# Mixture-of-experts code sum by an identity matmul and a two-part single-pass map, in a planned single-core kernel

## The chip, the core and the metric

The kernel runs on one core of a Trainium2 chip. The metric is the time of the whole program on the device in microseconds, as the median of several executions. The core has five engines with an instruction queue each: TensorE (PE in the profile, its weight loads PEld), VectorE (DVE), ScalarE (ACT), GpSimd (POOL) and SyncE (SP), which here only issues DMAs. Each queue is worked off in order, and the engines meet through semaphores.

## What is computed

Eight batches of 512 tokens with 256 features pass through four residual layers: a local attention A over 44 offsets, a feed-forward part F, a full causal attention B, and F again. The change touches F alone. Its core in the reference, with M = 64 code columns, E = 8 experts and H = 512:

```python
spikes_enc = jax.nn.sigmoid(inputs_embeds @ enc_W + enc_b)
cont = flat @ s2c_W + s2c_b
...
h = jax.nn.relu(jnp.einsum('nm,emh->enh', cont, We1) + be1[:, None, :])
expert_out = jnp.einsum('enh,ehm->enm', h, We2) + be2[:, None, :]
output_flat = jnp.einsum('enm,ne->nm', expert_out, gates)
spikes_moe = jax.nn.sigmoid(output_flat @ c2s_W + c2s_b).reshape(b, s, H)
decoded = jax.nn.sigmoid(spikes_moe @ dec_W + dec_b)
```

The gates are zero for all but two of the eight experts. The line with `c2s_W` is called "mapped to the code" here: 64 columns go to 512.

## The kernel before

**Calls.** A call is one stage for one batch: 8 calls of A, 8 of B and 16 of F. The attention calls run in the order A0, A1, B0, A2, B1, A3, and so on to B6, B7 (`calls`, from line 327). The F call with number n belongs to the n-th attention call and is interleaved with attention call n+1. So the F calls 1, 3, 5, 7, 9, 11 and 14 run beside a B call, as does 13; the F calls 0, 2, 4, 6, 8, 10 and 12 run beside an A call; F call 15 is the last and has nothing beside it.

**The order is planned.** `ordered()` simulates the engines with a price in us for each block of work (`p.put` in `local_phases`, `causal_phases`, `expert_phases`) and writes out one fixed queue for each engine. At each step it takes the block that can start first, within a tick of `TICK` us, and among equals the one with the least `urgency`: its offset of `PULL` and `CALL_PULL` less `DEPTH` times the length of the chain behind it. So these tables decide which call's work stands where on PE, DVE and ACT, and which of the eight PSUM banks each product gets.

**An F call.** The input x is normalised and transposed (`turn`), `enc` makes t_enc (tanh form of the sigmoid, four products of 128 rows), `cont` makes the 64 code columns twice, one copy in rows 0 to 63 and one in rows 64 to 127. ACT writes `cont` and `cont_hi`, which is `cont` in the type fp32r, and DVE writes `cont_lo = cont - cont_hi` (line 1434). The 16 `hid` products take two matmuls each, `(w, cont_hi)` and `(w, cont_lo)`; `we1` holds the rounded weights in its upper 64 rows and the rest of them in its lower 64. `eo` forms two experts at a time, one in each half of the 128 rows; DVE multiplies by the gates (line 1448) and adds up (line 1453) into `moe`, still two half sums, one above the other. `c2s` then is four products with plain fp32 operands, `c("c2s_w", n * P, P)` of 128 rows (the 64-row weights stacked twice, so that the two halves are added in the product) against `moe`; ACT takes the tanh (line 1170). `dec` (line 1800) starts when the four tanh tiles are there, 16 fp32 products in each of two banks; it ends in tanh, a second normalisation and the sum into x (`close`, lines 1470 and 1475).

**Setup.** Inside A0, DVE prepares constants (`setup_`, from line 1481): `split` makes the two parts of `we1` from `setup_pack`. Two packs of constants come by DMA at the start, `kept_pack` (stays) and `setup_pack` (lies in arena F until F call 0).

## Time and profile before

| what | value |
|---|---|
| median of 3 runs | 1747.21 us (1744.1 to 1747.36) |
| profiled execution | 1746.18 us, span 1743.3 us |
| PE busy | 1591.9 us, 91% |
| PEld busy | 895.6 us, 51% |
| DVE busy | 1285.2 us, 74% |
| ACT busy | 785.6 us, 45% |
| granted TensorE clock, mean | 0.98 |
| idle PE from 250 to 1450 us | 1200 - 1146.7 = 53.3 us |

The profiled execution lasts 2.9 us longer than its span, from the first to the last instruction. Busy time of PE is the union of its instructions, whose ends are modelled: they overlap, and the pace is read from one start to the next. In a row, the number in brackets after an instruction is the idle time of its engine just before it and what ended it. A product of two fp32 operands stands in the trace as two MATMUL instructions; one with fp32r operands as one.

### The profile page before, as it was taken

Reading aid. Unit: us, or ns where it says so; the run is one execution under the profiler, and the core shown is the slowest. Engines: PE = TensorE matmul, PEld = TensorE weight load, DVE = VectorE, ACT = ScalarE, POOL = GpSimd, SP = SyncE. Lnnn points to the kernel's source line nnn. Section 1 sums busy time; section 2 is a strip of 40 time slices with the busy share of each in tenths; the row PEclk is TensorE's granted clock in tenths of the full one; section 3 lists DMA queues with packets and bytes.
Section 4 is the critical chain, followed back from the end, with each engine's and each line's share of the span. In section 5 each row is a group of like instructions: output and inputs, shape, how many; then the busy total and the mean of one; then the engine's idle time right before and its main releaser. Section 6 shows DMA issues by size and latency. Waiting matters only on the chain. (4 is left out here: it accounts for less than half of the span.)

```text
span 1743.3 us, 28682 instructions
## 1 busy us (share of the span) xinstructions
PE 1591.9 (91%) x10784; PEld 895.6 (51%) x10800; DVE 1285.2 (74%) x3138; ACT 785.6 (45%) x1473; POOL 137.1 (8%) x155
## 2 busy tenths in 40 slices
PE   4689899999999989999999999999999998998976
PEld 2163564545555365554755456553655546454533
DVE  5969867896679866798668966898667985646723
ACT  1043445535364444644355353644436443563633
POOL 1020110001101020000100011010200001000000
PEclk9899999999999999999999999999999999998989
DMA  9040350014301152021600134001520216004000
GB/s 325 18 158 14 138 167 2 16 73 158 99 2 48 40 186 71 4 87 63 194 2 16 73 138 119 2 29 59 182 74 4 87 51 189 7 11 138 13 3 12
DMA packets 50262, 133.98 MB, mean 77 GB/s; under 512 B 6256, under 2 KB 22576, under 8 KB 45520
## 3 DMA queue, kind: packets, MB, share of 16 engines
q1 hardware_dynamic: 50128, 132.16, 23.0%
q8 instruction: 88, 1.44, 0.3%
q14 instruction: 46, 0.38, 0.1%
HBM read 80.99 MB, written 46.04 MB: 73 GB/s over the span
## 5 line engine op out<-in xcount | busy, mean ns | idle before, releaser
L1308 DVE TENSOR_TENSOR arena_AB<-qT,kT 128x2048 f32<-128x2048 f32 (+3 forms) x240 | 399.4, 1715 | 9.4 <-PE bank L1606 5.0
L1363 DVE CUSTOM_DVE_ANT_0 bank<-bank,causal_b 128x512 f32<-128x512 f32 (+3 forms) x512 | 233.6, 523 | 130.7 <-PE bank L1680 130.2
L1524 PE MATMUL bank<-arena_F,kept 128*128 128x512 f32 (+1 forms) x544 | 255.9, 615 | 13.9 <-DVE arena_F L1453 9.5
L1606 PE MATMUL bank<-arena_AB,slot_w 128*32 128x512 f32 x1408 | 200.0, 614 | 34.0 <-DVE arena_AB L1308 32.1
L1120 ACT ACTIVATE arena_AB<-bank 128x512 f32<-128x512 f32 (+1 forms) x352 | 166.9, 586 | 78.3 <-PE bank L1694 78.3
L1524 PEld LDWEIGHTS bank<-arena_F,kept 128*128 128x128 f32 (+1 forms) x544 | 99.6, 192 | 140.4 <-issue 117.1
L1153 ACT ACTIVATE arena_F<-bank,kept 128x512 f32<-128x512 f32 x256 | 160.4, 705 | 18.1 <-PE bank L1524 16.1
L1800 PE MATMUL bank<-kept,arena_F 128*128 128x256 f32 x512 | 116.2, 381 | 6.6 <-ACT arena_F L1170 6.6
L1785 PE MATMUL bank<-arena_F,kept 128*64 128x512 f32 x512 | 119.4, 600 | 2.2 <-ACT arena_F L1153 1.0
L1524 PE MATMUL bank<-xnT,kept 128*128 128x512 f32 x256 | 115.5, 604 | 4.4 <-ACT xnT L1045 2.7
L988 POOL TENSOR_TENSOR rstd_F<-var_eps_F,minus_half 128x4 f32<-128x4 f32 x32 | 34.3, 1072 | 971.3 <-DVE var_eps_F L1238 971.3
L1692 PE MATMUL bank<-arena_AB 99*128 99x256 bf16 (+3 forms) x512 | 110.2, 301 | 0.2
L1524 PE MATMUL bank<-cont_hi,we 128*128 128x512 f32 x256 | 108.6, 424 | 1.4 <-DVE arena_AB L1363 0.7
L1800 PEld LDWEIGHTS bank<-kept,arena_F 128*128 128x128 f32 x512 | 95.1, 189 | 25.9 <-ACT arena_F L1170 6.9
L1606 PEld LDWEIGHTS bank<-arena_AB,slot_w 128*32 128x32 f32 x1408 | 35.4, 109 | 133.2 <-DVE arena_AB L1308 86.6
L1524 PE MATMUL bank<-cont_lo,we 128*128 128x512 f32 x256 | 100.5, 393 | 0.0
L1711 PE MATMUL bank<-arena_AB,V_b 128*32 128x512 f32 (+3 forms) x1024 | 85.9, 438 | 10.5 <-ACT arena_AB L1120 7.6
L1694 PE MATMUL bank<-causal_T,ident_b 128*128 128x128 bf16 x512 | 95.2, 219 | 0.0
L1680 PE MATMUL bank<-arena_AB 96*128 96x512 bf16 (+3 forms) x512 | 85.7, 301 | 2.2 <-DVE arena_AB L1363 1.4
L1461 DVE TENSOR_TENSOR arena_F<-bank,kept 128x512 f32<-128x512 f32 x32 | 22.0, 688 | 88.5 <-PE bank L1800 88.5
L1071 ACT ACTIVATE arena_AB<-bank,kept 128x512 f32<-128x512 f32 (+1 forms) x48 | 33.6, 701 | 115.9 <-PE bank L1613 115.9
L1137 ACT ACTIVATE arena_F<-bank,half_enc_b 128x512 f32<-128x512 f32 x64 | 44.0, 687 | 92.1 <-PE bank L1524 92.1
(191 smaller groups left out, 2420.9 us busy)
## 6 DMA issues: line engine op xcount, KB each, us to landing
arena_AB<-band SPq DMA_DIRECT2D x32, 1344.0 KB, 6.4
arena_AB<-stacks SPq DMA_DIRECT2D x64, 384.0 KB
stacks<-arena_AB SPq DMA_DIRECT2D x48, 256.0 KB, 2.8
band<-arena_AB SPq DMA_DIRECT2D x32, 328.0 KB, 3.6
stacks<-xnT SPq DMA_DIRECT2D x32, 256.0 KB, 2.6
band<-kT SPq DMA_DIRECT2D x4, 1352.0 KB, 22.0
stacks<-xn SPq DMA_DIRECT2D x16, 256.0 KB, 2.4
kept<-kept_pack SPq DMA_DIRECT2D x1, 3797.0 KB, 18.7
```

The lines of the kernel that those rows point to most:

```text
L1120: nc.scalar.activation(p_T[:, n % RS, cols[0]:cols[-1] + 1, 0:w], ps[:, 0:len(cols) * w].rearrange("p (c q) -> p c q", c=len(cols)), ACT.E ...
L1153: nc.scalar.activation(hid[:, n % RH, :], ps[:], ACT.Relu, bias=c("be1", n, 1)).then_inc(read, 1)
L1308: ins = nc.vector.tensor_tensor(prod[SET_AT[i]][:, col:col + c, :], qT[:, hf, :].unsqueeze(1).broadcast_to([P, c, T]), k, ALU.mult)
L1363: ins = nc.vector.tensor_tensor_reduce(out=s, in0=s, in1=causal[:, (TT - 1 - i) * P:T], scale=-1.0, scalar=BIG, op0=ALU.add, op1=ALU.min, ...
L1524: ins = nc.tensor.matmul(out(ps), w, x, start=n == 0, stop=n == len(pairs) - 1)
L1606: ins = nc.tensor.matmul(ps[HS * col:HS * (col + 1), :], slot_w[:, slot(n), :], prod[SET_AT[i]][:, col, :], start=r == 0, stop=False, skip ...
L1680: ins = nc.tensor.matmul(ps[:, at:at + (i + 1) * P], stacks[0:K, h // 4, 0, h % 4, i * P:(i + 1) * P], stacks[0:K, h // 4, 1, h % 4, 0:(i ...
L1692: nc.tensor.matmul(ps[:, at * w:(at + 1) * w], stacks[0:K + 3, g, 1, col, k * P:(k + 1) * P], stacks[0:K + 3, g, 0, col, k * P:T], start=T ...
L1694: ins = nc.tensor.matmul(ps[:, at * w:at * w + P], ident_b[:], causal_T[:], start=False, stop=True, skip_group_check=True)
L1711: ins = nc.tensor.matmul(ps_o[HS * col:HS * (col + 1), k * P:T], V_b[:, k, columns_of(4 * g + col)], p_T[:, n % RS, col, 0:w], start=k == ...
L1785: ins = nc.tensor.matmul(ps[M * e:M * (e + 1), :], we2[:, 2 * n + e, k, :], hid[:, (4 * n + 2 * e + k) % RH, :], start=k == 0, stop=k == 1)
L1800: ins = nc.tensor.matmul(ps[:, i * D:(i + 1) * D], t_moe[:, k, at:at + P], dec_w[:, k, :], start=k == 0, stop=k == KF - 1)
```

## The change

- `c2s_w` moves from the pack that stays to the setup pack, behind `we1`. A new tile `by_cont` holds `we1` and `c2s_w` side by side, and `split` treats both: upper 64 rows rounded, lower 64 rows the rest.
- A new phase `both` stands before `c2s`. PE multiplies `moe` by `pair_sum`, a 128 x 128 matrix of four identities of 64, as a plain fp32 product; each half of the result holds the sum of the two half sums. ACT copies the result to `cont_hi` (fp32r), DVE subtracts: `cont_lo = result - cont_hi`.
- Each `c2s` product is now two matmuls with fp32r operands, `(w, cont_hi)` and `(w, cont_lo)`. The first waits until DVE has read the bank of `both`.
- `ones` moves to the end of arena F; two small additions of `ident` make `pair_sum` in the setup.
- The planner has the new blocks, and `TICK`, `DEPTH`, `PULL` and `CALL_PULL` are other numbers, so that the order of all stages is planned anew.

```diff
-    ("be1", 2 * E), ("we2", E * 2 * M), ("be2", E // 2), ("c2s_w", FF), ("c2s_b", KF),
+    ("be1", 2 * E), ("we2", E * 2 * M), ("be2", E // 2), ("c2s_b", KF),
...
-          ("causal_T", P), ("we1", E * EH)]
+          ("causal_T", P), ("we1", E * EH), ("c2s_w", FF)]
...
-        p.put(("c2s", m), ("PE", 0.86, ("eo", E // 2 - 1, "DVE")), ("ACT", 0.6))
+        if m == 0:
+            p.put("both", ("PE", 0.86, ("eo", E // 2 - 1, "DVE")), ("ACT", 0.6), ("DVE", 0.67))
+        p.put(("c2s", m), ("PE", 0.46, ("both", "DVE")), ("ACT", 0.6))
...
-TICK, DEPTH = 0.078, 0.23
+TICK, DEPTH = 0.02, 0.04
...
-    ("A", "ACT"): {"sT": 730},
-    ("A", "DVE"): {"prod": 2330},
-    ("A", "PE"): {"tS": 1545.8, "pA": -2110, "pr": -630},
-    ("B", "DVE"): {"S": 1140, "pr": 330},
-    ("B", "PE"): {"turn": 1070, "S": 2980, "ST": 590, "pr": 230},
-    ("F", "ACT"): {"hid": 1230},
-    ("F", "DVE"): {"lg": 2160, "eo": -1470},
-    ("F", "PE"): {"turn": 740, "hid": 983.2, "dec": 4990},
+    ("A", "ACT"): {"p": -40},
+    ("A", "DVE"): {"prod": 3260, "tS": 400, "pr": -850},
+    ("A", "PE"): {"prod": 590, "pA": 342.5, "on": 470, "oNT": 1520, "pr": 341},
+    ("B", "DVE"): {"S": 1010},
+    ("B", "PE"): {"v": 180, "S": 2390, "ST": 600},
+    ("F", "ACT"): {"hid": 630, "c2s": -2050},
+    ("F", "DVE"): {"lg": 460, "both": 1320},
+    ("F", "PE"): {"turn": 1890, "hid": 1070, "gb": -1370, "eo": -290, "c2s": 190, "dec": 6710},
...
-    "A": [-4050, 2690, 0, 0, -446.1, 0, 0, 0],
-    "B": [0, 0, 0, 0, 0, 0, -630, 0],
-    "F": [0, 0, 0, 0, 0, 0, 109.2, 0, 0, 0, 0, 0, 0, -1500, 0, 0],
+    "A": [-6150, 0, -860, 0, 0, 0, 0, 0],
+    "B": [0, 0, 0, 0, 0, 0, 0, -410],
+    "F": [-350, 0, 0, 0, 0, 0, 0, 0, 0, 0, 0, 0, 0, -570, 160, 0],
...
+                elif kind == "both":
+                    act.wait_ge(*bank_full(u, name))
+                    nc.scalar.copy(cont_hi, place(u, name)[0][:]).then_inc(sem["F"]["moe_hi_ready"], 1)
...
+                elif kind == "both":
+                    dve.wait_ge(*nth(u, "moe_hi_ready", 1))
+                    ps, read = place(u, name)
+                    nc.vector.tensor_tensor(cont_lo, ps[:], cont_hi.bitcast(fp32), ALU.subtract).then_inc(read, 1)
...
+                    for half in range(2):
+                        once(nc.vector.tensor_tensor(pair_sum[:, half * M:(half + 1) * M], ident[:, 0:M], ident[:, M:P], ALU.add))
...
-                    we1_flat, rounded = we1[:].rearrange("p e n -> p (e n)"), arena["F"][:, SETUP_W:SETUP_W + E * EH]
-                    once(nc.vector.tensor_copy(rounded.bitcast(fp32r), s_only("we1")))
-                    once(nc.vector.tensor_copy(we1_flat[0:M, :], s_only("we1")[0:M, :]))
-                    once(nc.vector.tensor_tensor(we1_flat[M:P, :], s_only("we1")[M:P, :], rounded[M:P, :], ALU.subtract))
+                    given, rounded = setup_only[:, S_W:SETUP_W], arena["F"][:, SETUP_W:2 * SETUP_W - S_W]
+                    once(nc.vector.tensor_copy(rounded.bitcast(fp32r), given))
+                    once(nc.vector.tensor_copy(by_cont[0:M, :], given[0:M, :]))
+                    once(nc.vector.tensor_tensor(by_cont[M:P, :], given[M:P, :], rounded[M:P, :], ALU.subtract))
...
+                elif kind == "both":
+                    pe.wait_ge(*nth(u, "moe_ready", 1))
+                    product(u, name, lambda ps: ps[:], [(pair_sum[:], moe)])
                 elif kind == "c2s":
                     if n == 0:
-                        pe.wait_ge(*nth(u, "moe_ready", 1))
-                    product(u, name, lambda ps: ps[:], [(c("c2s_w", n * P, P), moe)])
+                        pe.wait_ge(*bank_read(u, "both"))
+                    w = c2s_w[:, n * P:(n + 1) * P]
+                    product(u, name, lambda ps: ps[:], [(w, cont_hi), (w, cont_lo)])
```

## Rows read from the trace of the kernel before

**Rows 1.** The page, busy time, share and instructions of each engine.

```profile
PE 1591.9 (91%) x10784; PEld 895.6 (51%) x10800; DVE 1285.2 (74%) x3138; ACT 785.6 (45%) x1473; POOL 137.1 (8%) x155
```

**Rows 2.** Windows: length, busy PE, PEld, DVE, ACT, POOL (instructions), clock, DMA, GB/s.

```profile
250.00:1450.00 1200.00, 1146.71 (x7737) 646.40 (x7748) 930.72 (x2258) 575.01 (x1082) 91.99 (x97) 1.00 0.22 72
1450.00:1680.00 230.00, 203.61 (x1417) 118.24 (x1417) 143.34 (x509) 109.35 (x216) 12.61 (x15) 0.95 0.18 54
1680.00:1743.30 63.30, 44.74 (x154) 24.05 (x155) 18.24 (x48) 22.25 (x39) 1.01 (x1) 0.88 0.02 9
```

**Rows 3.** Groups by line and form: busy us, mean ns, idle before.

```profile
L1524 PE MATMUL bank<-arena_F,kept 128*128 128x512 f32 x512 | 238.8, 615 | 12.5 <-DVE arena_F L1453 9.5 <-issue 1.5 <-ACT arena_F L1045 1.4
L1434 DVE TENSOR_TENSOR cont_lo<-arena_F,cont_hi 128x512 fp32r<-128x512 f32 x16 | 10.9, 684 | 17.1 <-ACT cont_hi L1143 17.1
L1143 ACT ACTIVATE cont_hi<-bank,s2c_bias 128x512 fp32r<-128x512 f32 x16 | 10.9, 680 | 0.0
```

**Rows 4.** Windows, finished moe to first dec: F calls 4, 5, 14 and 15.

```profile
616.95:621.80 4.85, 3.70 (x9) 1.47 (x9) 4.25 (x10) 3.46 (x6) 0.58 (x1) 1.00 0.95 372
706.84:720.46 13.62, 13.28 (x101) 6.78 (x99) 9.35 (x41) 8.96 (x19) 0.00 (x0) 1.00 0.00 1
1624.10:1637.95 13.85, 13.74 (x97) 6.83 (x96) 13.71 (x60) 8.38 (x16) 0.00 (x0) 1.00 0.02 5
1719.88:1724.62 4.74, 3.71 (x9) 1.47 (x9) 0.00 (x1) 2.75 (x4) 0.00 (x0) 1.00 0.00 0
```

**Rows 5.** Timeline, F call 5: start, us, engine, line, instruction.

```profile
706.98 3.65 PE L1524 MATMUL bank<-arena_F,kept 128*128 128x512 f32 x8
...
710.47 0.33 PE L1692 MATMUL bank<-arena_AB 99*128 99x384 bf16 x1
```

**Rows 6.** Timeline, F call 4 beside A3, around its c2s.

```profile
614.11 1.44 PE L1581 MATMUL bank<-kept,arena_AB 128*128 128x128 f32 x12
...
617.00 3.70 PE L1524 MATMUL bank<-arena_F,kept 128*128 128x512 f32 x8 [1.45 <-DVE arena_F L1453]
617.35 1.08 DVE L1264 TENSOR_REDUCE arena_AB<-bank 128x8 f32<-128x352 f32 x2
...
621.80 3.71 PE L1800 MATMUL bank<-kept,arena_F 128*128 128x256 f32 x16 [1.09 <-ACT arena_F L1170]
625.34 1.97 PE L1626 MATMUL bank<-kept,arena_AB 128*128 128x128 f32 x16
```

**Rows 7.** Timeline, F call 0, two hid products.

```profile
184.01 0.50 PE L1524 MATMUL bank<-cont_hi,we 128*128 128x512 f32 x1
...
184.34 0.39 PE L1524 MATMUL bank<-cont_lo,we 128*128 128x512 f32 x1
...
184.57 0.40 PE L1524 MATMUL bank<-cont_hi,we 128*128 128x512 f32 x1
...
184.83 1.27 ACT L1153 ACTIVATE arena_F<-bank,kept 128x512 f32<-128x512 f32 x2 [1.02 <-PE bank L1524]
```

**Rows 8.** Timeline, F call 15: c2s, its first tanh, first dec.

```profile
1719.94 3.70 PE L1524 MATMUL bank<-arena_F,kept 128*128 128x512 f32 x8 [1.62 <-DVE arena_F L1453]
...
1721.10 0.69 ACT L1170 ACTIVATE arena_F<-bank,half_c2s_b 128x512 f32<-128x512 f32 x1 [4.94 <-PE bank L1524]
...
1724.62 7.17 PE L1800 MATMUL bank<-kept,arena_F 128*128 128x256 f32 x32 [0.98 <-ACT arena_F L1170]
```

**Rows 9.** Timeline, F call 15: from cont_hi to cont_lo.

```profile
1698.04 0.68 ACT L1143 ACTIVATE cont_hi<-bank,s2c_bias 128x512 fp32r<-128x512 f32 x1
...
1698.82 0.69 DVE L1434 TENSOR_TENSOR cont_lo<-arena_F,cont_hi 128x512 fp32r<-128x512 f32 x1 [17.07 <-ACT cont_hi L1143]
```

**Rows 10.** Timeline, setup: the three instructions of split.

```profile
89.00 1.23 DVE L1497 CAST arena_F<-arena_F 128x2048 fp32r<-128x2048 f32 x1
...
90.27 1.52 DVE L1498 CAST we<-arena_F 64x2048 fp32r<-64x2048 f32 x1
...
91.82 2.59 DVE L1499 TENSOR_TENSOR we<-arena_F 64x2048 fp32r<-64x2048 f32 x1
```

More of the change, by code:

```diff
@@ L446, in fills_of @@
     if stage == "F":
-        reader = "DVE" if kind in ("lg", "eo", "dec") else "ACT"
+        reader = "DVE" if kind in ("lg", "eo", "dec", "both") else "ACT"
         return [phase], reader
@@ L606 @@
 ATTN_SETUP = 11
-DVE_SETUP = 26
+DVE_SETUP = 28
 PARITY = ("_even", "_odd")
@@ L655, in build @@
         cont_lo = sb("cont_lo", [P, T], fp32r)[:]
-        we1 = sb("we1", [P, E, EH], fp32r)
+        by_cont = sb("by_cont", [P, E * EH + FF], fp32r)
+        we1 = by_cont[:, 0:E * EH].rearrange("p (e n) -> p e n", e=E)
+        c2s_w = by_cont[:, E * EH:E * EH + FF]
         rh = sb("rh", [P, T])
         gT = sb("gT", [P, T], bf16)
+        pair_sum = sb("pair_sum", [P, P])
         V = sb("V", [P, TT, VW])
@@ L750, in build @@
         setup_only = arena["F"][:, 0:SETUP_W]
+        ones = arena["F"][:, ARENA["F"] - P:ARENA["F"]]
         Norm = namedtuple("Norm", "xn xnT stats mv var rstd scrap")
```

5 lines of the change are left out of this document (2 added, 3 removed).

## The prediction, before the result was known

> **What bounds the kernel now.** I read the busy shares first. PE leads with 91% against 74% for DVE and 45% for ACT [rows 1]. A share is only an average, so the windows came next. From 250 to 1450 us PE is busy 1146.7 of 1200 us, which is 95.6%, at a granted clock of 1.00 [rows 2]; DVE has 930.7 us there. The reader is to see that two thirds of the program are held by PE with 53 us of small holes in them, and that the last 63 us, in which F call 15 runs alone, are another thing: PE busy 44.7 of 63.3 us, DVE 18.2, ACT 22.3 [rows 2]. There each step waits for the one before, and what counts is the length of the chain.
>
> The Trainium skill, "Perfetto Trace Analysis", section "Identifying the Most-Contended Engine", says that the busy share of matmuls is a poor measure of how near TensorE is to its limit, and asks for the busy share of weight loads instead; that is 51% here. Taken alone it would say that half of PE is free.
>
> Then I looked at the place of the change in all 16 calls, from the moment at which `moe` is complete to the first `dec`. There are two kinds, and the last call. **Covered calls**: in F call 5 PE is busy 13.28 of 13.62 us [rows 4]; `c2s` is followed at once by scores of B [rows 5], and `dec` comes 10 us later. Calls 3, 7, 9 and 11 look the same, calls 1 and 13 nearly so, and call 0 has the transposes of A1 in between: eight calls. Call 14 is covered too, but there DVE is full with 13.71 of 13.85 us [rows 4]. **Open calls**: in F call 4 PE waits 1.45 us in its queue for `moe`, runs `c2s`, waits again 1.09 us for the tanh tiles and runs `dec` [rows 6]; the window is 4.85 us long with 3.70 us of PE [rows 4]. Calls 2, 6, 8, 10 and 12 look the same: six calls. Call 15 has a window of 4.74 us with 3.71 us of PE [rows 4, 8].
>
> **Pace and prices.** The eight MATMULs of `c2s` last from 706.98 to the next product at 710.47, 3.49 us or 0.87 us for a plain fp32 product of 512 columns [rows 5]; the mean of 615 ns for one MATMUL [rows 3] is longer than the pace because they overlap. A matmul with fp32r operands follows the last at 184.57 - 184.34 = 0.23 us, the first of a group takes 0.33 us [rows 7]. So PE loses 3.49 us per call and gets 0.87 us for `both` and 8 x 0.23 + 0.1 = 1.94 us for the new `c2s`: 2.81 us, **0.68 us less per call**, 10.9 us in 16 calls. DVE gets 0.68 us and ACT 0.68 us per call, at the prices of `cont_lo` and `cont_hi` [rows 3]; ACT's copy might be some 0.1 us cheaper, which changes nothing.
>
> **The new waits.** PE now cannot go from `moe` to `c2s` directly. From the start of `both` to ACT is 1721.10 - 1719.94 = 1.16 us [rows 8]; from ACT to DVE 1698.82 - 1698.04 = 0.78 us, DVE 0.69 us [rows 9], and 0.06 us to PE, as from the end of `moe` at 1719.88 [rows 4, 8]. `c2s` starts 2.69 us after `both`. Its first tanh starts 184.83 - 184.01 = 0.82 us later [rows 7] and four of 0.69 us follow [rows 8], because PE now delivers every 0.46 us and ACT needs 0.69. With 0.25 us to PE, `dec` can start 2.69 + 0.82 + 2.76 + 0.25 = 6.5 us after `both`, against 1724.62 - 1719.94 = 4.7 us now [rows 8]: **1.8 us more of chain**. In it PE has two holes, 2.69 - 0.87 = 1.8 us before `c2s` and 6.5 - 2.7 - 1.9 = 1.9 us after it. Queued behind the waiting `both` on DVE is whatever the plan puts there: maxima of B's scores in covered calls, in open calls the softmax of A (two reductions start at 617.35, half a microsecond after `moe` [rows 6]), on ACT the exponentials of the same stage. A copy placed too early holds those up, placed too late it lengthens the hole.
>
> **Covered calls, eight:** B's scores and weightings are there to fill both holes, as they fill the 10 us before `dec` today. I take the full 0.68 us less 0.05 us for one more change between kinds of matmul, -0.63 x 8 = **-5.0 us**. The bounds are nothing gained and -0.7 each. In call 14 DVE gets as much as PE loses; I take 0, bounds +0.7 and -0.7.
>
> **Open calls, six:** PE has 3.7 us of holes where it has 1.1 us now. If nothing fills them, the call costs +1.8 us, the chain's own growth. The next work of A in the queue is a set of transposes of 1.97 us, at 625.34, directly behind the first half of `dec` [rows 6]; its data comes by DMA, so it may be ready for the second hole and not for the first. If it fills the second hole, the sum is 3.7 - 1.9 - 1.1 - 0.68 = 0.0 us. If the transposes of 1.44 us at 614.11 [rows 6] also go into the first hole, it is -1.4 us, but the softmax that waits for them is on A's way through the DMA. The offsets are set anew, so the plan has a chance at all of it; I take -0.3 us each, near the middle case, **-1.8 us**, with bounds -8.4 and +10.8.
>
> **Call 15:** nothing lies beside it, **+1.8 us**, taken in full.
>
> **Setup:** `split` works on 2560 columns instead of 2048: a quarter more of 1.23 + 1.52 + 2.59 = 5.34 us is +1.3 us on DVE [rows 10], and two additions of 64 columns add about 0.3 us. It stands ahead of a softmax of A0 and PE has little else then; I take **+1.2 us**, bounds 0 and +1.6. The move of 256 KB from one pack to the other costs nothing: the sum of the bytes ahead of the setup is the same, and DVE reads this pack at 89.00 with no idle time before it [rows 10]. Were it late, 262 kB at the 372 GB/s of rows 4 would be 0.7 us. `ones` in arena F and the names cost nothing; `both` holds one of eight banks 2.7 us, which only the plan feels.
>
> **The offsets anew:** they move the work of every stage. The trace cannot show their effect. The 53 us of holes in the middle [rows 2] bound what they can give, and one hole more or less of 1 us in each of eight rounds makes 8 us either way. I take 0 and keep -8 and +8.
>
> **Sum:** -5.0 + 0 - 1.8 + 1.8 + 1.2 = -3.8 us on the profiled execution's 1746.18 us, 1742.4 us. The median of the runs stands 1.0 us above that execution and the fastest run 2.1 us below, so I leave the median at 1742.4 us, 0.3% less than 1747.21. About 0.2%, 3.5 us, is what a measurement of this kernel can tell from no change.
>
> **Rivals.**
> *All holes filled* (chance 0.24): the plan finds work for both holes of the open calls. -0.68 x 8 - 1.4 x 6 + 3.0 = -10.8, about 1735 us. For it: PE is at 95.6% already with a fixed plan. Against: the open calls have a hole of 1.1 us that nothing fills today, although 2 us of transposes stand behind `dec` [rows 6].
> *Open holes stay open* (0.16, the other side): no work of A is ready between `both` and `dec`, six calls cost 1.8 us each. -5.0 + 10.8 + 3.0 = +8.8, about 1755 us. It decides from the point at which the band's DMA lands later than 4.5 us after `both`. DMA is at 0.95 in just this window [rows 4], which speaks for it.
> *PE's saving does not reach the end* (0.14): in the covered calls DVE and ACT, which get 0.68 us each and are busy 9.35 and 8.96 of 13.62 us [rows 4], hold the pace, and PE only idles longer. -1.8 + 3.0 = +1.2, about 1748 us. The rule of the skill named above points this way. The trace speaks against it: PE stands idle 0.34 of 13.62 us there [rows 4], starts follow each other without a gap at 0.43 us per fp32 MATMUL, and a weight load lies under a running matmul.
> *The clock falls* (0.03): in the last 63 us the mean granted clock is 0.88, that is 63.3 x 0.12 x 2 = 15 us at 1.2 GHz [rows 2], which cost up to 7.6 us; PE had stood idle before the calls' chain there. If a hole of 1.8 us did the same in each open call at half that price, +23 us, about 1765 us. The windows of rows 4 say 1.00 with 1.1 us holes. The Trainium skill, "TensorE: Matmul & The Clock Gate", section "A second HAM failure mode: psum-queue depth-cycling", describes small idles between groups of matmuls that make the clock swing; the trace shows no such swing at the present holes.
> *The two parts are no single passes* (0.02): if the new matmuls ran at 0.43 us instead of 0.23, 128 of them would cost 25 us more, about 1767 us. The `hid` products of the same types at 0.23 us [rows 7] exclude nearly all of it.
>
> **How the numbers follow.** The forecast, 1742.4, has the remaining 0.41; by the offsets' bounds its own range is 1734 to 1750. For 8 in 10 I reach to the filled case and into the open one: 1730 to 1755. Faster by over 0.2% means under 1743.7: all of the filled case and some two thirds of the forecast, less where its offsets turn out badly, 0.53. Within 0.2%, 1743.7 to 1750.7: a quarter of the forecast and most of the third rival, 0.24. Slower: open holes, clock, passes and a bad plan, 0.23.
>
> **What would show it.** New rows for `pair_sum` x32 MATMULs and for `c2s` x128 at a pace of 0.23 us; PE's busy time lower by some 11 us; in covered calls B's matmuls between `both` and `c2s`; in open calls A's transposes between `c2s` and `dec`; in call 15 6.5 us from `both` to `dec`; `split` at 6.7 us. PE idle between 250 and 1450 us well above 53 us would make it wrong, and so would a softmax of A that waits behind `both` on DVE.

## The result and the profile after

The changed kernel takes 1775.37 us (median of 4 runs, 1772.95 to 1779.09), the kernel before, beside it, 1747.28 us: a ratio of 1.0157 with an interval of 1.0137 to 1.0177. It is 28 us slower, where 1742.4 us was forecast, and it lies outside the range of 1730 to 1755. The profiled execution took 1779.09 us with a span of 1777.1 us.

The busy times, from the page of after, beside [rows 1]:

```profile
PE 1605.2 (90%) x10816; PEld 913.9 (51%) x10832; DVE 1300.1 (73%) x3156; ACT 794.5 (45%) x1489; POOL 139.7 (8%) x155
```

The matmuls are 32 more, as they should be (32 for the pair product; 128 single ones in place of 128 halves of fp32 products). PE's busy time should have fallen by 11 us. It rose by 13.3 us. The middle window of after, beside [rows 2] (length, busy time of PE, PEld, DVE, ACT and POOL, granted clock, DMA share, GB/s):

```profile
250.00:1450.00 1200.00, 1133.84 (x7621) 643.91 (x7631) 926.71 (x2248) 568.17 (x1068) 91.17 (x94) 0.98 0.21 68
```

From 250 to 1450 us PE is idle for 66.2 us where it was 53.3, which was one of the signs named as making the prediction wrong. And the granted clock is 0.98 where it was 1.00 [rows 2]. Read in windows of 50 us, the stretch has some 37 us at 1.2 GHz where it had 7; the whole execution has 1777.1 x (1 - 0.969) x 2 = 110 us of it, where it had 70. PE's busy time grows because the same matmuls last longer.

The new groups of after (busy us, mean ns, idle before), beside [rows 3]:

```profile
L1538 PE MATMUL bank<-arena_F,pair_sum 128*128 128x512 f32 x32 | 18.6, 664 | 13.7 <-DVE arena_F L1461 7.4 <-DMA arena_AB<-band 6.3
L1538 PE MATMUL bank<-cont_hi,by_cont 128*128 128x512 f32 x320 | 139.0, 434 | 5.3 <-DVE cont_lo L1469 3.5 <-DVE arena_AB L1371 1.3
L1469 DVE TENSOR_TENSOR cont_lo<-bank,cont_hi 128x512 fp32r<-128x512 f32 x16 | 11.0, 688 | 11.5 <-ACT cont_hi L1174 11.4
L1174 ACT CAST cont_hi<-bank 128x512 fp32r<-128x512 f32 x16 | 9.6, 599 | 35.8 <-PE bank L1538 35.8
```

PE now stands idle 13.7 us ahead of the 16 pair products; ahead of the old `c2s` it was 9.5 us, the part of the 12.5 us of [rows 3] that ended with the last addition (L1453). So this stall has moved to `both` and has grown. DVE's subtraction costs 0.69 us, as forecast, and ACT's copy 0.60 us, the 0.1 us less that the prediction had thought possible.

**A covered call of after**, F 5, timeline, beside [rows 5]:

```profile
718.03 1.07 PE L1538 MATMUL bank<-arena_F,pair_sum 128*128 128x512 f32 x2
719.15 0.58 ACT L1174 CAST cont_hi<-bank 128x512 fp32r<-128x512 f32 x1 [0.26 <-PE bank L1538]
719.76 0.69 DVE L1469 TENSOR_TENSOR cont_lo<-bank,cont_hi 128x512 fp32r<-128x512 f32 x1 [1.92 <-ACT cont_hi L1174]
720.70 0.48 PE L1538 MATMUL bank<-cont_hi,by_cont 128*128 128x512 f32 x1
...
722.41 0.39 PE L1538 MATMUL bank<-cont_lo,by_cont 128*128 128x512 f32 x1
...
726.80 3.71 PE L1818 MATMUL bank<-kept,arena_F 128*128 128x256 f32 x16
```

`c2s` starts 2.67 us after `both` and PE has work of B in between, `c2s` lasts 722.41 - 720.70 + 0.23 = 1.94 us. The prediction had 2.69 and 1.94.

**An open call of after**, F 6 beside A4, PE and DVE; F 4 of before stands in [rows 6]:

```profile
828.07 0.83 PE L1595 MATMUL bank<-kept,arena_AB 128*128 128x128 f32 x6
830.99 1.12 PE L1538 MATMUL bank<-arena_F,pair_sum 128*128 128x512 f32 x2 [2.09 <-DMA arena_AB<-band]
833.26 3.65 PE L1640 MATMUL bank<-kept,arena_AB 128*128 128x128 f32 x16 [1.14 <-issue]
834.07 1.09 DVE L1272 TENSOR_REDUCE arena_AB<-bank 128x8 f32<-128x352 f32 x2 [3.13 <-DMA band<-arena_AB]
836.06 0.68 DVE L1469 TENSOR_TENSOR cont_lo<-bank,cont_hi 128x512 fp32r<-128x512 f32 x1
836.80 0.80 PE L1538 MATMUL bank<-cont_hi,by_cont 128*128 128x512 f32 x1
837.39 0.63 PE L1538 MATMUL bank<-cont_lo,by_cont 128*128 128x512 f32 x1
...
841.18 7.17 PE L1818 MATMUL bank<-kept,arena_F 128*128 128x256 f32 x32 [1.14 <-ACT arena_F L1178]
```

From `both` to `dec` it is 10.2 us, where the prediction's chain had 6.5. F 6 is one of the two longest: the six open calls take 7.3, 7.8, 10.2, 8.3, 10.2 and 8.6 us here, and 4.6 to 4.8 in before. Three things are to be seen. PE stands idle 2.09 us ahead of `both`; the row names a DMA, but the band read had nothing to do with `both`, which waits for DVE's last addition (it ended at 830.94). On DVE the softmax of A (L1272) stands ahead of the low part (L1469) and itself waits 3.13 us for a DMA, so the high part, ready at 832.73, lies unused for 3.3 us. PE meanwhile waits 1.14 us for A's band and then transposes it (L1640); `c2s` stands behind these transposes in its queue. And the passes of `c2s` last 0.63 us where they last 0.39 in F 5, and the next one starts 0.43 us later, not 0.23: PE runs at half its clock.

Read over whole calls, from the first `enc` tile to the last tanh, the open call F 6 and the covered call F 7, first before, then after:

```profile
776.80:836.40 59.60, 57.24 (x322) 28.86 (x322) 45.73 (x64) 27.56 (x49) 3.20 (x4) 1.00 0.25 90
876.30:931.90 55.60, 54.88 (x302) 30.77 (x305) 39.51 (x146) 30.35 (x59) 0.00 (x0) 1.00 0.01 2
```

```profile
786.00:849.80 63.80, 59.04 (x317) 31.04 (x317) 44.74 (x61) 28.60 (x51) 3.08 (x4) 0.95 0.24 88
892.70:948.70 56.00, 54.68 (x305) 30.60 (x308) 39.00 (x142) 30.90 (x59) 0.00 (x0) 1.00 0.01 3
```

The open call grew by 4.2 us, with 0.05 x 63.8 x 2 = 6.4 us at 1.2 GHz in it; the covered one, which has 0.68 us of matmuls less, did not shrink.

**The round.** From F 4 to F 12 the program repeats a round of one open call, A, one covered call and B, four times. Each number below is the mean of the four rounds, between the same instructions' ends in each kernel's trace: the round, the open call and the covered call (first `enc` tile to last tanh), PE's idle time, and the time at 1.2 GHz.

| kernel | round | open | covered | PE idle | 1.2 GHz |
|---|---|---|---|---|---|
| before | 204.1 | 59.0 | 55.8 | 9.2 | 1.7 |
| filled_holes_before | 203.4 | 59.0 | 55.8 | 9.3 | 0.0 |
| after | 209.4 | 62.7 | 55.7 | 11.8 | 8.5 |
| new_sum_old_order | 209.0 | 64.0 | 56.2 | 11.0 | 10.2 |
| filled_holes_old_order | 205.7 | 61.1 | 56.1 | 8.5 | 0.0 |
| split_in_covered_only | 203.8 | 59.1 | 56.1 | 9.5 | 0.0 |
| split_without_first | 203.8 | 59.1 | 56.1 | 9.4 | 0.0 |
| covered_passes_alone | 202.4 | 59.1 | 54.5 | 9.4 | 0.9 |
| old_sum_new_order | 207.2 | 61.3 | 55.7 | 10.7 | 3.4 |
| old_sum_in_place | 210.3 | 60.8 | 60.0 | 11.6 | 6.8 |
| old_sum_write_first | 210.4 | 64.5 | 55.7 | 13.1 | 6.8 |
| write_before_read | 209.3 | 64.0 | 55.8 | 13.1 | 6.0 |
| low_part_first | 209.9 | 63.2 | 55.7 | 12.9 | 6.0 |
| filled_holes_new_order | 207.6 | 62.0 | 55.7 | 9.1 | 0.9 |
| filled_holes_both_moves | 208.7 | 62.9 | 55.9 | 10.5 | 0.9 |
| new_sum_old_offsets | 215.8 | 67.4 | 60.5 | 16.7 | 13.7 |

In these rounds filled_holes_before is the program of before, unchanged, so the first two rows show how far two executions of one program differ: 0.7 us a round, with 1.7 us at 1.2 GHz in one and none in the other. At the first `enc` tile of F 2 the same two already differ by 2.6 us (369.4 and 372.0 us).

Of the 5.3 us by which the round of after is longer, 3.7 are in the open call, 0.9 between it and the next covered call, 0.8 between the covered call and the next open one, and -0.1 in the covered call. From F 2 to F 14 this makes 30.6 of the 33.8 us that the span grew; 1.8 had come before and 1.4 come after.

### The profile page after: what moved, and what is told of

It reads as the page before. It is cut to its first block and busy times, and to the rows that moved or that the text cites. A ratio compares the mean times of both kernels' runs of the same rounds, so it can differ in the third digit from the quotient of the medians.

```text
span 1777.1 us, 28781 instructions
## 1 busy us (share of the span) xinstructions
PE 1605.2 (90%) x10816; PEld 913.9 (51%) x10832; DVE 1300.1 (73%) x3156; ACT 794.5 (45%) x1489; POOL 139.7 (8%) x155
## 5 line engine op out<-in xcount | busy, mean ns | idle before, releaser
L1538 PE MATMUL bank<-arena_F,kept 128*128 128x512 f32 (+1 forms) x416 | 195.4, 615 | 3.7 <-issue 1.4
L1538 PE MATMUL bank<-cont_hi,by_cont 128*128 128x512 f32 x320 | 139.0, 434 | 5.3 <-DVE cont_lo L1469 3.5
L1538 PE MATMUL bank<-cont_lo,by_cont 128*128 128x512 f32 x320 | 128.0, 400 | 0.0
L1538 PEld LDWEIGHTS bank<-arena_F,kept 128*128 128x128 f32 (+1 forms) x416 | 76.0, 192 | 101.0 <-issue 93.5
```

The source lines that it names most:

```text
L1538: ins = nc.tensor.matmul(out(ps), w, x, start=n == 0, stop=n == len(pairs) - 1)
```

## Experiments

### The two halves of the change apart

**new_sum_old_order**: the new arithmetic in the order of before. The queue of PE is that of before, with the pair product where `c2s` stood and the new `c2s` behind as much other work as covers 1.8 us, where there is any before `dec`.

```diff
-TICK, DEPTH = 0.02, 0.04
+TICK, DEPTH = 0.078, 0.23
...
-ORDER, FILLS = ordered()
+ORDER, FILLS = with_both()
```

> The changed arithmetic (identity sum, two parts, single-pass map) in the order that the kernel before has: PE keeps its old sequence except that the new product takes the old place of the first c2s product and the four c2s products come after the next 1.8 us of work, or directly where dec is next; the other engines keep their old priorities. My theory (the loss comes from the new order, in which the write of A's second tile is issued after the 1.3 MB read of its first one and lands late, not from the arithmetic): 1744 to 1756 us, at most 0.5% over the kernel before, and the second band write lands in about 2.2 to 3.5 us. The rival (the longer chain moe, high part, low part, c2s itself costs the 28 us): 1770 us or more.

**old_sum_new_order**: the fp32 sum of before with the offsets and in the order of after, the pair product left out of it.

```diff
-ORDER, FILLS = ordered()
+ORDER, FILLS = without_both()
```

> The arithmetic of the kernel before (four plain fp32 products, no extra phase) in the order of the changed kernel, engine by engine, with the extra phase taken out. My theory (the order is what costs): 1770 to 1790 us, and the second band write of the calls A2 to A7 lands after 4.5 us or more, as in the changed kernel. The rival (the arithmetic's chain is what costs): within 10 us of 1747.

Measured: 1781.62 us for the new sum in the old order, ratio 1.0206 (1.0182 to 1.0231), and 1773.56 us for the old sum in the new order, 1.0156 (1.0136 to 1.0177). The first misses my theory, the second meets it. The two halves don't add up to the 28 us: each alone costs about as much as both together. So there are at least two mechanisms, and the arithmetic alone has one of them. The timeline of F 6 in new_sum_old_order shows it, and behind it the windows ahead of and from 840.90:

```profile
839.06 1.13 PE L1566 MATMUL bank<-arena_F,pair_sum 128*128 128x512 f32 x2 [1.00 <-DVE arena_F L1489]
842.12 0.80 PE L1566 MATMUL bank<-cont_hi,by_cont 128*128 128x512 f32 x1 [1.94 <-DVE cont_lo L1497]
...
846.84 5.38 PE L1846 MATMUL bank<-kept,arena_F 128*128 128x256 f32 x14 [0.93 <-issue]
```

```profile
840.90:851.10 10.20, 8.05 (x18) 5.97 (x19) 3.09 (x7) 4.21 (x6) 0.00 (x0) 0.50 0.69 271
831.00:840.90 9.90, 8.19 (x46) 4.20 (x44) 9.45 (x19) 5.55 (x10) 3.20 (x4) 1.00 0.42 137
```

Nothing of A stands between `both` and `dec` in PE's queue. PE is idle 1.00 us, then 1.94 us. Within the second hole, at 840.9, the clock falls from 2.4 to 1.2 GHz and stays there for 10.2 us, in which 8.05 us of matmuls run that at 2.4 GHz would take half of it. In this kernel's trace each of the six open calls has 6.8 to 10.2 us at 1.2 GHz.

### Queue order inside the changed order

**write_before_read** takes up the 3.13 us of DVE in F 6: SyncE issues the band read of block 0 (1344 KB) ahead of the second write, on which the softmax's own transfer depends. The move puts the write first, as before has it. **low_part_first** moves the low part ahead of that softmax on DVE.

```diff
+def write_first():
...
+    of = ORDER["SP"]
+    for u in ATTENTION:
+        if u.stage == "A":
+            of.remove((u, ("read", 0)))
+            of.insert(of.index((u, ("write", 1))) + 1, (u, ("read", 0)))
...
+def low_part_first():
...
+    of = ORDER["DVE"]
+    for u in EXPERT_CALLS:
+        at = of.index((u, "both"))
+        if of[at - 1][1] == ("tS", 3):
+            of[at - 1], of[at] = of[at], of[at - 1]
```

> The changed kernel with one move in SP's queue in the calls A2 to A7: the read of the first band comes after the write of the second tile, as in the kernel before. My theory (the write stands behind the read's 1.3 MB in the DMA rings, the softmax of the fourth tile waits for it on DVE, and the low part stands behind that): the write lands in 2.2 to 3.5 us instead of 4.4 to 7.3, the wait of DVE for it goes, 3 us less in each of six calls, 1750 to 1762 us. The rival (the wait is only passed on, to the read that now starts 2.3 us later): 1772 to 1780 us.

> The changed kernel with one move in DVE's queue in the open calls: the subtraction that makes the low part stands ahead of the softmax of the fourth tile instead of behind it. If DVE's waiting in order holds up c2s: c2s starts some 3 us earlier in five or six calls, 1755 to 1766 us. If the band's write itself is what counts: A still waits for it, 1770 to 1778 us.

Measured: 1782.7 us, 1.0204 (1.0182 to 1.0227), and 1784.59 us, 1.0213 (1.0193 to 1.0232). Both are slower than the changed kernel and above both of their expectations. In low_part_first the low part does come early, but `c2s` doesn't (F 6, DVE and PE):

```profile
838.34 0.69 DVE L1481 TENSOR_TENSOR cont_lo<-bank,cont_hi 128x512 fp32r<-128x512 f32 x1 [1.84 <-ACT cont_hi L1186]
839.69 3.62 PE L1652 MATMUL bank<-kept,arena_AB 128*128 128x128 f32 x16 [2.00 <-issue]
842.96 0.61 PE L1550 MATMUL bank<-cont_hi,by_cont 128*128 128x512 f32 x1
```

The low part ends at 839.03 and lies unused for 3.9 us, because A's transposes `pA` (L1652) stand ahead of `c2s` on PE, and they wait for the band read, which landed 9.0 us after its issue at 830.58. From `both` to `dec` it is 10.2 us as before the move. That the low part was late is true in the trace of after and was not what the time hung on. In write_before_read DVE's wait of 3.13 us is gone in F 6, and PE's wait ahead of `pA` is 2.69 us instead of 1.14.

**old_sum_write_first** is the first move on old_sum_new_order:

> The fp32 sum of before in the changed order (old_sum_new_order, 1773.6 us), with each attention call A's second band write queued ahead of its first band read, as in before. Theory 'the queue order costs': the write no longer stands behind a 1344 KB read, tS(3) comes 2 to 3 us earlier in A 2 to A 7, 1760 to 1766. Rival 'the read, started later, only passes the wait on': 1771 to 1778.

1789.67 us, 1.0241 (1.0226 to 1.0255), 16 us more than without the move, and against both of its expectations. The row that tells why, the transposes `pA` of F 6's neighbour A4, in old_sum_new_order and then in old_sum_write_first:

```profile
833.83 2.72 PE L1642 MATMUL bank<-kept,arena_AB 128*128 128x128 f32 x16 [1.93 <-issue]
```

```profile
841.67 3.31 PE L1654 MATMUL bank<-kept,arena_AB 128*128 128x128 f32 x16 [4.83 <-issue]
```

In the changed order `pA` of block 0 stands in PE's queue ahead of `c2s` and `dec`. It needs the band read, and so all of PE waits for what stands ahead of this read in SyncE's queue. The read lands as fast as before (`pA` starts 6.6 us after its issue at 835.10, and 6.4 us after 827.44 without the move), but it is issued 41.1 us after the call's first `enc` tile instead of 38.4, because the second write must first have its data: PE's wait is 4.83 us instead of 1.93. In the order of before `pA` stands behind the first half of `dec` [rows 6] and can come late. The queue order of SyncE in after was thus right for its own PE order, and my reading of DVE's wait had picked the wrong one of two waits.

### Keeping the clock by filling the holes

**filled_holes_old_order** and **filled_holes_new_order** put matmuls that nothing reads into the holes; nothing else changes.

```diff
+            def keep_busy(u, name):
...
+                for _ in range(FILLER.get((u, name), 0)):
+                    nc.tensor.matmul(place(u, name, full)[0][:], ident, c("wk"), start=True, stop=True)
...
                     if n == 0:
+                        if FILLER.get((u, name)):
+                            pe.wait_ge(*bank_free(u, name))
+                            keep_busy(u, name)
                         pe.wait_ge(*bank_read(u, "both"))
```

> The new arithmetic in the order of before, as in new_sum_old_order (1781.6 us; span 1785.8), with TensorE's holes filled: 29 more fp32 products of 512 columns (identity times a constant weight, 0.87 us each) whose results nothing reads, two between the pair product and the first product to the code and two between the last of these and the decoder in calls F 2, 4, 6, 8, 10, 12 and 15, one in F 0. Nothing of the computation is left out. Theory 'clock': new_sum_old_order spent 42 us of TensorE's busy time at half clock in the stretches that begin in these calls (424.5, 632.7, 840.9, 1052.5, 1264.1, 1472.4 us), which is 21 us lost, and before has 3.4 us of such time there; with the holes filled the clock stays, the decoder's first half is back from 5.8 to 3.7 us, and the time is 1757 to 1768. Theory 'hand-offs': the time goes to PE -> ACT -> DVE -> PE alone, the half clock is a by-product in time that nobody waits for: 1779 to 1785, the half-clock stretches gone or not.

> The changed kernel with 35 such products that nothing reads: in F 2, 4, 6, 8, 10, 12 two ahead of the pair product (hole of 2.09 us there in F 6), one between it and the first product to the code, two ahead of the decoder; four in F 15 and one in F 0. Nothing of the computation is left out. Theory 'clock': the stretches at half clock of after at 624, 832, 860, 1044, 1252 and 1280 us hold 32 us of busy time, 16 us lost; without them 1759 to 1767. Theory 'hand-offs and queue order': the holes are waits for VectorE and for the band's transfer, which the filling doesn't shorten: 1773 to 1781.

Measured: 1773.63 us, 1.0149 (1.0128 to 1.017), against 1781.62 without filling, and 1767.69 us, 1.0117 (1.0092 to 1.0143), against 1775.37. In both pairs 8 us come back by work that has no use, 10 if each is read against the kernel before that ran beside it (34 us over it, then 24; 28, then 18). F 6 in filled_holes_old_order, and its whole call there beside the same call of new_sum_old_order:

```profile
833.75 1.13 PE L1589 MATMUL bank<-arena_F,pair_sum 128*128 128x512 f32 x2 [1.00 <-DVE arena_F L1507]
834.71 1.88 PE L1580 MATMUL bank<-kept 128*128 128x512 f32 x4
836.82 0.50 PE L1589 MATMUL bank<-cont_hi,by_cont 128*128 128x512 f32 x1 [0.23 <-DVE cont_lo L1515]
...
838.78 1.88 PE L1580 MATMUL bank<-kept 128*128 128x512 f32 x4
840.49 3.63 PE L1875 MATMUL bank<-kept,arena_F 128*128 128x256 f32 x16
```

```profile
789.30:850.90 61.60, 59.98 (x332) 30.72 (x332) 46.34 (x64) 28.02 (x50) 3.21 (x4) 1.00 0.25 93
```

```profile
794.60:859.40 64.80, 60.62 (x324) 31.71 (x323) 46.33 (x64) 28.28 (x50) 3.20 (x4) 0.92 0.24 89
```

L1580 is the filling. With it the clock is 1.00 instead of 0.92 and the call 3.2 us shorter; from `both` to `dec` it takes 6.74 us instead of 7.78. Over a round the time at 1.2 GHz goes from 10.2 us to nothing and the round is 3.4 us shorter (the table, before rounding). From `both` to `dec` the six open calls take 6.7 to 6.8 us: with the clock held, the chain has the length that was forecast, 6.5, and nothing of A lies in it. The spans of the two profiled executions differ by 14.1 us, the medians by 8.0: the profiled one of new_sum_old_order was the longest of its four (1787.82 us), with the lowest mean clock, so how often the clock falls differs from one execution to the next. The times lie between the two expectations in both orders: above theory 'clock' (1757 to 1768 and 1759 to 1767, the second by under 1 us) and below its rival. The clock is a part only, and with it held 24 and 18 us remain. Of the 28.4 us of span that filled_holes_old_order has over before, 8.3 come up to F 2, 12.4 from there to F 14 (1.6 us in each of the four rounds of the table) and 7.7 behind it. In the last part this execution has 8.4 us at 1.2 GHz within F 14, which no filling was laid for, and F 14 is 3.7 us longer than without filling.

**filled_holes_both_moves** repeats both moves with the clock held.

> filled_holes_new_order (1767.7 us) with both moves at once: the second band write ahead of the first band read, and the low part ahead of tS(3) on VectorE. Single moves without filling were slower than the changed kernel (1782.7, 1784.6), with the clock at half for 111 and 99 us. Theory 'they were hidden by the clock and by one another': with the clock held the pair product is answered 3 us earlier in six open calls, 1750 to 1760. Rival 'what they bring is lost behind tS(3) and the later band read': 1765 to 1775.

1782.63 us, 1.02 (1.0185 to 1.0214), 15 us more than filled_holes_new_order. This agrees with old_sum_write_first and lies above both expectations: with the clock held, the moves still cost.

**filled_holes_before** is the same trick on the kernel before, ahead of the last two calls.

> The kernel before with 14 products of 0.87 us that nothing reads: seven ahead of F 14's first transposes (hole of 6.90 us), five ahead of F 15's (5.61 us), one ahead of F 15's first product to the code and one ahead of its decoder. Theory 'clock': the encoder's 16 MATMULs that took 8.58 and 9.73 us at half clock take about 6.9, and the time is 1741 to 1745. Theory 'clock costs nothing that is waited for': 1746 to 1749.

1745.73 us, 0.9983 (0.9968 to 0.9998), with 10 runs: between its two expectations, and at the edge of what can be told from no change. The encoder's 16 MATMULs in F 14, then in F 15, in before and in filled_holes_before:

```profile
1586.50 8.58 PE L1524 MATMUL bank<-arena_F,kept 128*128 128x512 f32 x16 [0.72 <-issue]
...
1683.19 9.73 PE L1524 MATMUL bank<-arena_F,kept 128*128 128x512 f32 x16 [0.68 <-ACT arena_F L1045]
```

```profile
1587.39 8.80 PE L1532 MATMUL bank<-arena_F,kept 128*128 128x512 f32 x16 [0.77 <-ACT arena_F L1048]
...
1685.01 7.13 PE L1532 MATMUL bank<-arena_F,kept 128*128 128x512 f32 x16 [0.73 <-ACT arena_F L1048]
```

In F 15 the filling kept the clock (7.13 us, 2.6 less); in F 14 seven products were there too and did not.

### The covered calls by themselves

**split_in_covered_only** has the new arithmetic in eight calls that have a stage beside them, in the order of before; the other calls make one fp32 product of the weights as they lie in `by_cont`, so their code is another one, for the same work. **split_without_first** is the same with seven of the eight calls. **covered_passes_alone** has the eight single passes there and leaves out pair product, copy and subtraction.

```diff
-product(u, name, lambda ps: ps[:], [(w, cont_hi), (w, cont_lo)])
+product(u, name, lambda ps: ps[:], [(w, cont_hi), (w, cont_lo)] if u.nth in SPLIT
+        else [(w.bitcast(fp32), moe)])
```

> The new arithmetic in calls F 0, 1, 3, 5, 7, 9, 11 and 13 alone, where a part of stage B lies between the pair product and the products to the code; the other eight calls multiply the two half sums in fp32 in one step, as before, in the order of before. Its weights there are the high and the low part, not the full weight twice, so the code of those eight calls is another one; the work is that of before. My theory: what open calls lost (hand-offs, clock) is gone, and TensorE's 0.68 us less per covered call reaches the end in part: 1741 to 1746. Rival 'saving does not arrive': the covered phases end when ACT or VectorE are done, 1746 to 1750. Rival 'also the covered calls lose' (their VectorE step stands ahead of stage B's work): 1752 or more.

> split_in_covered_only with F 0 back to the one fp32 step: the new arithmetic in F 1, 3, 5, 7, 9, 11 and 13 alone (in the other calls the code is another one, as there; the work is that of before). In split_in_covered_only a call F 1, 3, .. took 0.36 us longer than in before from its encoder to its last tanh (56.13 against 55.77), although TensorE has 0.68 us less to do, and it was 9 us behind before after F 0 and A 1 already (253.5 against 244.5). My theory: the seven covered calls give nothing (between -0.3 and +0.4 us each), and F 0 with A 1 costs 3 to 9 us by its hand-off and the half clock behind it: 1742 to 1748. Rival 'covered calls lose': 1750 to 1753.

> The kernel before, its order and its waits, but the four products to the code in F 0, 1, 3, 5, 7, 9, 11 and 13 are the eight single passes of the new arithmetic and start with the half sums' end: no pair product, no cast, no subtraction (left out; the code is another one in all calls). TensorE has 1.55 us less to do in each of the eight calls (3.49 against 1.94), 12.4 us in all. Theory 'TensorE's saving reaches the end in covered calls': 1735 to 1739. Rival 'banks and ACT pace the covered stretch' (split_in_covered_only: passes 0.25 to 0.43 us apart instead of 0.23, score products then 0.28 instead of 0.23): half of it or less arrives, 1741 to 1748.

Measured: 1751.38 us, 1.0014 (1.0002 to 1.0026); 1747.95 us, 1.0003 (0.9993 to 1.0013); 1740.52 us, 0.9957 (0.9944 to 0.997). The first lies between two of its expectations, with 1749.98 us for before beside it. The second meets my theory by its time, at the theory's upper end, though F 0 had been put at 3 to 9 us there. The third got 7.4 of its 12.4 us (1747.93 us for before) and lies between its two expectations.

The first run also tells where the loss is. new_sum_old_order has the same order and differs from it by the new arithmetic in the other eight calls, F 2, 4, 6, 8, 10, 12, 14 and 15. It is 33.9 us over the kernel before beside it, and split_in_covered_only is 1.4 us over. So 32.5 of the 33.9 us hang on these eight calls. All but F 14 have nothing of another stage between `both` and `dec` in this order, and the clock falls in them. The whole call F 7 in split_in_covered_only and in covered_passes_alone, beside 55.60 us in before:

```profile
884.30:940.20 55.90, 55.02 (x304) 30.66 (x307) 40.32 (x147) 31.00 (x60) 0.00 (x0) 1.00 0.01 2
```

```profile
876.50:930.90 54.40, 53.50 (x305) 30.50 (x308) 39.62 (x147) 30.27 (x58) 0.00 (x0) 1.00 0.01 2
```

In the mean of four rounds the passes alone, 1.55 us less of PE, make the covered call 1.26 us shorter (54.5 against 55.8): in this stretch PE's time is the call's time, four fifths of it arrive. The pair product and the hand-offs then add 1.6 us (56.1), of which the pair product is 0.91 us on PE. The rest is in F 5 of split_in_covered_only:

```profile
718.16 0.47 PE L1571 MATMUL bank<-cont_hi,by_cont 128*128 128x512 f32 x1
718.47 0.40 PE L1571 MATMUL bank<-cont_lo,by_cont 128*128 128x512 f32 x1
...
719.05 0.40 PE L1571 MATMUL bank<-cont_lo,by_cont 128*128 128x512 f32 x1
719.48 0.50 PE L1571 MATMUL bank<-cont_hi,by_cont 128*128 128x512 f32 x1
...
720.28 0.39 PE L1571 MATMUL bank<-cont_lo,by_cont 128*128 128x512 f32 x1
```

The passes start 0.31 us apart, then up to 0.43 us, and the eight take 720.28 + 0.23 - 718.16 = 2.35 us, not 1.94. With the pair product's 0.91 us that is 3.26 us, 0.23 less than the 3.49 of [rows 5] instead of 0.68. Another 0.4 us goes in B's scores ahead of `dec`: the last of them begin 2.69 us before `dec` in before (717.77) and 3.08 us before it here (725.38), with gaps of up to 0.27 us from one start to the next. That the products wait for banks which ACT and DVE have still to read is what these starts suggest; no other assignment of banks was tried.

By the medians F 0 makes a difference of 1.4 us against the kernel before beside each; the intervals of 1.0014 and 1.0003 overlap. In the traces F 0 is 67.1 us long with the new arithmetic and 63.4 without, has a hole of 1.24 us ahead of `c2s`, and its neighbour A1 runs partly at 1.2 GHz. Over the seven other calls the profiled rounds come out 0.3 us shorter than in before (203.8 against 204.1), but the second execution of the same program has 203.4, and the difference between the two lies in A's stretch and its time at 1.2 GHz. Against that one, with no time at 1.2 GHz in either, the round is 0.4 us longer, as the covered call is.

### What the new order costs

**old_sum_in_place** keeps the changed order but has the old `c2s` where the pair product stands.

```diff
-    fixed = {e: [x for x in of if x[1] != "both"] for e, of in order.items() if e != "DMA"}
+    for u in EXPERT_CALLS:
+        at = pe.index((u, "both"))
+        pe[at:at + 1] = [(u, ("c2s", m)) for m in range(KF)]
```

> The fp32 sum of before in the changed order, but its four products stand where the changed kernel has the pair product, not where it has the products to the code: in F 2, 4, .. 12 ahead of the band's transposes pA of the stage beside them, in covered calls some 5 us earlier. VectorE and ACT keep the changed order's ranks. In old_sum_new_order (1773.6 us) the sum of F 6 was complete at 833.4 and its products began at 836.35, behind pA, which waited for the band's transfer until 833.83. Theory 'the place behind pA costs': the changed order is made for a sum that is still on its way through ACT and VectorE, and each open call loses 3 us by it; in place it is back: 1752 to 1762. Rival 'the changed order costs elsewhere' (the later second band write, the softmax tS(3)): 1768 to 1776.

**new_sum_old_offsets** is the other end: the new arithmetic, and `PULL`, `CALL_PULL`, `TICK` and `DEPTH` of before.

> The new arithmetic with the offsets of before, unchanged, and the order that these give by themselves (not before's order, which new_sum_old_order kept). Theory 'an order stands and falls with its offsets': the two added steps shift every later choice, more of TensorE's holes than in new_sum_old_order (1781.6) and more time at half clock, 1795 to 1825. Rival 'offsets are of little weight beside the hand-offs': 1773 to 1785.

Measured: 1779.95 us, 1.0169 (1.0147 to 1.019), and 1823.18 us, 1.0419 (1.0397 to 1.0441). The second is within my theory. The first is above both of its expectations, and my theory of the place behind `pA` falls: the open calls gained 0.5 us each by it (60.8 against 61.3), not 3, for F 6 lost the rest in another way (timeline of old_sum_in_place):

```profile
836.56 5.40 PE L1546 MATMUL bank<-arena_F,kept 128*128 128x512 f32 x8 [2.09 <-DVE arena_F L1475]
```

The same 2.09 us stand ahead of `both` in after, and 1.00 us in new_sum_old_order, whose order is that of before. Of the 1.09 us between them, 0.6 is that six of A's transposes stand in PE's queue ahead of `both` (0.83 us in the rows of after) where the old order has twelve (1.44 us, as in [rows 6]), and 0.5 is that the half sums are complete later against the end of PE's `eo`. Behind this hole the clock falls in this kernel too (5.40 us for products that take 3.70 at full clock). The covered calls lose 4.3 us there, since B's order was laid for a `c2s` 5 us later. Why the plan lays the additions and the transposes so was not taken apart further. The second run shows what the renewal of the offsets was worth: 1.0419 against 1.0157, some 46 us, where the change of arithmetic could give 10.9 by its own sum.

## Why the prediction was wrong

The forecast had -3.8 us. This is what the terms became, each as the difference between the profiled executions of after and before (spans, +33.8 us; medians, +28):

| term | forecast | measured |
|---|---|---|
| six open calls | -1.8 | +18.4 |
| eight covered calls (F 1 alone: +3.7) | -5.0 | +3.2 |
| call 14 | 0 | +1.3 |
| call 15 | +1.8 | +3.8 |
| ahead of F 0's first `enc` tile | +1.2 | +0.8 |
| between the calls and behind the last (offsets) | 0 | +6.3 |

**PE's and the other engines' prices: right, but for the setup.** `c2s` at 1.94 us, the pair product at 0.91 (0.87 was forecast), DVE 0.69, ACT 0.60, 2.67 us from `both` to `c2s` where nothing stands between; `split` took 1.49 + 1.79 + 3.13 = 6.4 us. The setup as a whole cost more than its bound of 1.6: the first `enc` tile of F 0 ends at 143.4 us in both executions of before's program and at 145.3 to 145.7 in the five kernels with the new setup in the old order, 2 us. The rows of `split` in after:

```profile
89.97 1.49 DVE L1511 CAST arena_F<-arena_F 128x2560 fp32r<-128x2560 f32 x1
...
93.32 3.13 DVE L1513 TENSOR_TENSOR by_cont<-arena_F 64x2560 fp32r<-64x2560 f32 x1
```

**Covered calls: the step "B's scores and weightings are there to fill both holes", -5.0 us, failed.** In the order of before the call got 0.3 to 0.4 us longer instead of 0.63 shorter; eight such calls gave +1.4 us, seven nothing that can be told from no change. In after itself they stayed as they were (55.7 against 55.8). I had priced the hand-offs at 0.05 us per call because the holes are filled. Filled they are; yet the pair product and its two readers on ACT and DVE cost 1.6 us over the passes alone, and the passes of 0.23 us do not keep their pace. This is the rival "PE's saving does not reach the end", to which I gave 0.14, but its mechanism is narrower than I had put it: by covered_passes_alone a saving without hand-offs does reach the end. The rule of the Trainium skill in "Perfetto Trace Analysis", "Identifying the Most-Contended Engine", which judges PE by the busy share of its weight loads, would by this share alone have had half of PE free. PEld is busy 30.7 of 55.9 us in this stretch, and still PE's work set its length.

**Open calls: the step "I take -0.3 us each, near the middle case" failed, and it weighs most.** The middle case had A's transposes fill the second hole. They fill neither in the old order, and in the new one they come with a wait of their own: each open call of after is 3.1 us longer on average, 18.4 in all. With the clock held, the call costs +2.0 us in the old order and +3.0 in the new one. In the old order it is the rival "open holes stay open" with its own price, 1.8 us each, to which I gave 0.16. In the new one the transposes do stand in the first hole, as I had hoped for the best case; but their band read is waited for there, and the softmax ahead of the low part waits too. The hole ahead of `both`, which the sum left out, also grew, from 1.00 us to 2.09 in F 6. I had seen that this softmax starts half a microsecond after `moe`, and had named it as what would make the prediction wrong, without a price.

**The clock: the rival at 0.03 was a main part.** I had argued that windows with 1.1 us holes show 1.00. They do. With a second hole of 1.9 us each of the six open calls of new_sum_old_order has time at 1.2 GHz; in after four of the six have 3.4 to 6.8 us of it, and F 2, with the same 2.09 us ahead of `both`, has none, so the length of that hole alone doesn't decide it. The mean clock of F 6 fell to 0.95 in after and 0.92 in new_sum_old_order; filling alone brought 8 us back in both orders. The Trainium skill, "TensorE: Matmul & The Clock Gate", "A second HAM failure mode: psum-queue depth-cycling", describes clock swings by idles between groups of matmuls. Its direction agrees with the open calls, where idles of 1.00 and 1.94 us went with a fall to 1.2 GHz. My +23 us for it was too much for a part that sits on top of the chain's growth, and too little in its chance.

**Call 15: +1.8 us, measured +3.8** (45.6 to 49.4 us from `enc` to the last tanh). The waits are as forecast, 2.53 us to `c2s`; but it too runs at 1.2 GHz behind its holes (beside [rows 8]; the window runs from `both` to `dec`):

```profile
1748.84 1.12 PE L1538 MATMUL bank<-arena_F,pair_sum 128*128 128x512 f32 x2 [1.64 <-DVE arena_F L1461]
1751.37 0.79 PE L1538 MATMUL bank<-cont_hi,by_cont 128*128 128x512 f32 x1 [1.40 <-DVE cont_lo L1469]
1755.93 9.62 PE L1818 MATMUL bank<-kept,arena_F 128*128 128x256 f32 x32 [0.78 <-ACT arena_F L1178]
```

```profile
1748.84:1755.93 7.09, 4.91 (x11) 2.78 (x11) 0.69 (x1) 3.33 (x5) 0.00 (x0) 0.63 0.00 0
```

7.09 us instead of 6.5, and `dec` itself 9.62 instead of 7.17 us [rows 8]. With its holes filled the call took 47.3 us in the old order and 46.1 in the new one.

**Offsets: 0 with a bound of 8 us either way.** This bound, taken from the holes of before, doesn't hold for an order in general: the old sum in the new order costs 26 us, and the new sum with the old offsets 73. The holes that are there limit what an order can gain, not what it can lose. For the changed kernel the term has no number of its own, because it depends on what the order is laid on: beside the new sum in the old order the new order is 6 us better (1775.37 against 1781.62), within the bound, and beside the old sum 26 us worse.

**What stays open.** With the clock held and the new sum, the new order still costs 2 us a round more than the old one (207.6 against 205.7), 1.0 of it in the open call, by the two waits, and 0.8 between the covered call and the next open one; of the latter I have no cause. The changed kernel is nonetheless 6 us faster than new_sum_old_order: their rounds are alike (209.4 and 209.0), and the other is 6.0 us later at F 2 already, 4.2 of them within F 0 (66.5 against 62.3 us). Why the mean clock differs between executions of one kernel was not tried.

## What to carry to other kernels

Price a new hand-off between engines where nothing lies beside it and where something does, and count in both cases the work that it pushes back in each queue; a matmul saving smaller than the hand-off's own length is a loss until shown otherwise. When an edit lengthens a hole of PE, look at the granted clock behind the holes of that length that the trace already has, and test by filling them with matmuls that nothing reads. A fixed order belongs to its arithmetic: exchange either alone, as an experiment, before the cause is sought in the other. Where an engine's queue holds two late things in a row, taking the first wait away shows only the second: look for what stands next in the queue before a move is tried.

## What the runs showed of the hardware

Matmuls that nothing reads can make a kernel faster: 29 and 35 of them, 25 and 30 us of PE time, brought 8 us each. Two idles of 1.00 and 1.94 us with 0.9 us of matmuls in between went with 10.2 us at 1.2 GHz, which began 0.7 us into the second, while 1.45 and 1.09 us around 3.7 us of matmuls [rows 6] did not. Ahead of F 15 five filling products (4.45 us) kept the encoder at 7.13 us where it had taken 9.73; ahead of F 14 seven (6.17 us) did not, with 8.80 against 8.58.
